# Cross attention: scores of two head pairs issued together between two projections; the last reciprocals pair by pair

## What is computed

```python
q = (x @ Wq).reshape(B, N, 8, 64).transpose(0, 2, 1, 3)          # B = 8, N = 128
k = (context @ Wk).reshape(B, M, 8, 64).transpose(0, 2, 1, 3)    # M = 2048
v = (context @ Wv).reshape(B, M, 8, 64).transpose(0, 2, 1, 3)
attn = softmax(einsum('bhnd,bhmd->bhnm', q, k) * 64 ** -0.5, axis=-1)
out = einsum('bhnm,bhmd->bhnd', attn, v)
out = out.transpose(0, 2, 1, 3).reshape(B, N, 512)
return out @ Wo + bo
```

## Time and profile before

| | |
|---|---|
| median of 3 runs | 1626.52 us (1625.01 to 1626.78) |
| profiled execution, its own time | 1637.39 us |
| its span | 1635.5 us |
| TensorE matmul busy | 1560.3 us, 95% of the span |
| TensorE weight load busy | 1225.8 us, 75% |
| GpSimd busy | 722.9 us, 44% |
| ScalarE busy | 694.3 us, 42% |
| VectorE busy | 630.8 us, 39% |
| mean granted TensorE clock | 0.983 of full speed |

### The profile page before, as it was taken

How to read it: one execution, slowest core, us unless ns; L and a number is a source line. 1 busy time by engine, 2 the same in 40 slices (tenths; PEclk the granted TensorE clock), 3 DMA queues, 4 the chain that set the end, 5 groups by cost and what they waited for, 6 DMA issues and landing times. The chain is left out here.

```text
span 1635.5 us, 25132 instructions
## 1 busy us (share of the span) xinstructions
PE 1560.3 (95%) x10022; PEld 1225.8 (75%) x10023; DVE 630.8 (39%) x951; ACT 694.3 (42%) x1132; POOL 722.9 (44%) x563
## 2 busy tenths in 40 slices
PE   7999999999999999999999999789899969999997
PEld 5677877877878878877877877734467747877876
DVE  4135435434434533533633632641644522222222
ACT  3244544544544544544544543414344403453522
POOL 3113913922931931941841850436200175588651
PEclk9999999999999999999999999999999989999999
DMA  5111021021021021020020110051000465556521
GB/s 206 58 52 59 1 85 57 3 84 44 16 85 33 27 85 33 27 84 31 29 85 26 33 66 27 1 205 64 23 1 1 149 212 135 149 160 191 158 39 35
DMA packets 56164, 116.90 MB, mean 71 GB/s; under 512 B 11072, under 2 KB 15232, under 8 KB 56064
## 3 DMA queue, kind: packets, MB, share of 16 engines
q1 hardware_dynamic: 46480, 98.17, 18.2%
q0 software_dynamic: 4816, 8.41, 2.7%
q10 hardware_dynamic: 4768, 8.91, 1.8%
HBM read 94.19 MB, written 22.33 MB: 71 GB/s over the span
## 5 line engine op out<-in xcount | busy, mean ns | idle before, releaser
L281 POOL TENSOR_TENSOR ctx_l<-stage,ctx_h 128x1024 fp32r<-128x1024 f32 x62 | 147.1, 2393 | 505.4 <-ACT ctx_h L616 505.3
L343 PE MATMUL ps_p<-wv,ctx_h 128*128 128x512 f32 x1024 | 329.3, 403 | 9.5 <-DVE ctx_l L686 9.3
L343 PE MATMUL ps_p<-ctx_h,wk 128*128 128x512 f32 x1024 | 336.2, 397 | 0.0
L724 DVE TENSOR_TENSOR s_top<-ps_s,s_top 128x512 f32<-128x512 f32 x192 | 123.5, 685 | 348.2 <-ACT s L589 348.2
L343 PEld LDWEIGHTS ps_p<-wv,ctx_h 128*128 128x128 f32 x1024 | 185.1, 189 | 56.2 <-issue 10.0
L343 PEld LDWEIGHTS ps_p<-ctx_h,wk 128*128 128x128 f32 x1024 | 192.2, 188 | 44.6 <-issue 2.9
L343 PE MATMUL ps_p<-wv,ctx_l 128*128 128x512 f32 x512 | 201.1, 393 | 0.0
L343 PE MATMUL ps_p<-ctx_l,wk 128*128 128x512 f32 x512 | 199.7, 390 | 0.0
L571 ACT ACTIVATE vt<-ps_p 128x512 f32<-128x512 f32 x128 | 76.4, 597 | 260.6 <-PE ps_p L343 199.4
L565 ACT ACTIVATE kT<-ps_p 128x512 f32<-128x512 f32 x128 | 76.4, 597 | 225.9 <-PE ps_p L343 142.3
L589 ACT ACTIVATE s<-ps_s 128x512 f32<-128x512 f32 x256 | 138.1, 598 | 52.2 <-PE ps_s L396 52.2
(11 more groups left out here) (252 smaller groups left out, 2291.7 us busy)
## 6 DMA issues: line engine op xcount, KB each, us to landing
stage<-in_ctx_dram SPq DMA_DIRECT2D x64, 512.0 KB, 3.9
raw_u<-in_up_dram SPq DMA_DIRECT2D x32, 512.0 KB
stage<-in_down_dram SPq DMA_DIRECT2D x16, 512.0 KB
raw_e<-in_down_dram SPq DMA_DIRECT2D x16, 512.0 KB
rows_scratch<-wxo SPq DMA_DIRECT2D x25, 256.0 KB, 2.6
wxo<-rows_scratch ACTq DMA_DIRECT2D x23, 256.0 KB
s<-in_x_dram SPq DMA_DIRECT2D x2, 1024.0 KB, 11.1
q_scratch<-s SPq DMA_DIRECT2D x2, 1024.0 KB, 4.5
```

Source lines behind the costliest of these rows:

```text
L281: nc.gpsimd.tensor_tensor(lo, raw, hi, ALU.subtract).then_inc(done, 1)
L343: mm = nc.tensor.matmul(out, w(c), m(c), start=(c + k == 0), stop=(c == DC - 1 and k == 2))
L724: ins = nc.vector.tensor_tensor(top[:, p, e], bank, top[:, p, e], ALU.max)
```

## The change

TensorE's `keys_and_scores` and `values_and_scores` take pairs two at a time: two score blocks, then two projections. ScalarE's functions follow. In `keys_and_scores` the scores now also come ahead of the projections. For the last sequence, `sums_of_chunks` writes into `ps_s`, `sums` of heads 0 to 3 is issued after pair 2, and VectorE takes the reciprocals in three steps.

```diff
+            def late_place(h):
+                return ps_s[h % 2 * XD:(h % 2 + 1) * XD, h // 2, 0:T]
...
             def sums_of_chunks(p):
                 for t in range(MT):
                     for h in (2 * p, 2 * p + 1):
-                        nc.tensor.matmul(sum_place(h), ones, s[:, h, t, :], start=(t == 0), stop=(t == MT - 1))
+                        mm = nc.tensor.matmul(late_place(h), ones, s[:, h, t, :], start=(t == 0), stop=(t == MT - 1))
+                mm.then_inc(late_done, 1)
...
             def keys_and_scores(b, g, also=None):
-                for p in range(PAIRS):
-                    project_k(b, g, p)
-                    scores(b, g - 1, p)
-                    if also:
-                        also(p)
+                for q in (0, 2):
+                    for p in (q, q + 1):
+                        scores(b, g - 1, p)
+                    for p in (q, q + 1):
+                        project_k(b, g, p)
+                        if also:
+                            also(p)
 
             def values_and_scores(b, g, also=None):
-                for t in range(4):
-                    scores(b, g, t)
-                    project_v(b, g, t)
-                    if also:
-                        also(t)
+                for q in (0, 2):
+                    for p in (q, q + 1):
+                        scores(b, g, p)
+                    for t in (q, q + 1):
+                        project_v(b, g, t)
+                        if also:
+                            also(t)
...
                 values(LASTB, p)
                 if p >= PAIRS // 2:
                     sums_of_chunks(p)
-            sums(LASTB, range(XH // 2))
+                if p == PAIRS // 2:
+                    sums(LASTB, range(XH // 2))
...
-            output(LASTB)
+            dve.wait_ge(l_done, B)
+            dve.wait_ge(o_stored, 16 * LASTB)
+            nc.vector.reciprocal(on[:, 0:PAIRS // 2, :].rearrange("p h t -> p (h t)"), ps_m[:, 0:PAIRS // 2 * T])
+            for p in range(PAIRS // 2, PAIRS):
+                dve.wait_ge(late_done, p - PAIRS // 2 + 1)
+                ins = nc.vector.reciprocal(on[:, p, :], ps_s[:, p, 0:T])
+            ins.then_inc(r_done, 1)
+            dve.wait_ge(r_done, B)
+            dve.wait_ge(pv_done, B * PAIRS)
+            nc.vector.tensor_tensor(on[:, :, :], ps_o[:, :, :], on[:, :, :], ALU.mult).then_inc(on_done, 1)
```

More of the change, by code:

```diff
@@ L165, in cross_attention @@
         l_done = sem("l_done")
+        late_done = sem("late_done")
         r_done = sem("r_done")
@@ L598, in keys_and_scores @@
             def keys_and_scores(b, g, also=None):
[L599 to L603, removed]
-            def values_and_scores(b, g):
-                for t in range(4):
-                    copy_score(b, g, t)
-                    copy_v(b, g, t)
+                for q in (0, 2):
+                    for p in (q, q + 1):
+                        copy_score(b, g - 1, p)
+                    for p in (q, q + 1):
+                        copy_key(b, g, p)
+                        if also:
+                            also(p)
+            def values_and_scores(b, g):
+                for q in (0, 2):
+                    for p in (q, q + 1):
+                        copy_score(b, g, p)
+                    for t in (q, q + 1):
+                        copy_v(b, g, t)
             def round_ctx(b, ks):
```

## The result

| | median | lowest to highest | ratio to before, 95% interval |
|---|---|---|---|
| before | 1626.65 us | 1625.01 to 1627.98 (4 runs) | |
| changed | 1600.05 us | 1599.48 to 1601.19 (4 runs) | 0.9838 [0.9821, 0.9855] |

The change saves 26.6 us; forecast were 27.2, and a time of 1599.3. The profiled execution of the changed kernel took 1599.48 us, its span 1597.6 us.

The account below looks back on a forecast made before the run. TensorE, busy 1560 of 1635.5 us, was taken as the bound. Savings of 24.1 + 1.3 + 1.35 + 0.4 = 27.2 us from the median 1626.5 gave 1599.3 us, range 1596 to 1608.

Parts of the forecast that it names:

- The gap of a run: Cross attention, TensorE: joining two score blocks saves 0.43 us; 56 joins give 24.1 us.
- The seam behind the values: Seven sequences, scores right behind values matmuls: seam costs 0.15 instead of 0.33 us, saving 1.3 us (0 to 2.3).
- the rule beside it: The Trainium skill's rule that changing tiling mode drains TensorE; by it the values seam saves zero, the sum 1.3 us less.
- The score banks: A pair fills all four banks of `ps_s`; they are emptied with at least 1.9 us spare, costing nothing.
- The tight place: First group: ScalarE's copy of pair 3 waits for GpSimd's last tree; TensorE spared by 0.9 us, cost nothing.
- Rivals A and C: A: tree delay passes cover, 14 us given back, 1613, chance 0.10; C: emptying becomes the bound, 1635, chance 0.03.
- The start of the last softmax: Last sequence: VectorE's first subtraction starts 1.1 us before the transposes instead of 0.27 after, saving 1.35 us.
- Sums and reciprocals: Last sequence: VectorE owes 128 reciprocal elements, not 512, against a new 2.1 us TensorE wait; saves 0.4 us.
- Rival E: Clock falls in the new wait before the last sequence's sums: up to 7.6 us, 1607; counted within the forecast's 0.80.
- Rival B: The gap is partly the recording's: joins give only 12 us, the sum is 15, time 1611; chance 0.05.

Follow-up runs that it names:

- full_pairs: The changed kernel with score matmuls over all 128 rows of keys and queries instead of row halves: 1684.31 us, against 1625.50 for the kernel before.
- fours: The changed kernel with four score blocks, then four value projections, in values_and_scores: 1651.86 us, ratio 1.0156 to the kernel before.
- tree1_after: The changed kernel with one more addition in GpSimd's last tree of each of seven sequences: 1598.05 us, against 1625.12 for the kernel before.
- tree4_after: The changed kernel with four more additions in GpSimd's last tree of each of seven sequences: 1609.82 us.
- tree4_before: The kernel before with four more additions in GpSimd's last tree of seven sequences: 1634.24 us against 1635.94 for the kernel before, ratio 0.999.
- sums_later: The changed kernel with the last sequence's sums of heads 0 to 3 behind the values of pair 3: 1607.02 us, ratio 0.9826 to the kernel before.
- after_again: The changed kernel unaltered, timed again on the slower chip: 1609.12 us against 1635.94 for the kernel before, ratio 0.9841.
- tail_only: The kernel before, score blocks single, with only the changed end of the last sequence (reciprocals in steps, sums after pair 2): 1625.89 us, ratio 1.000.
- keys_first: The changed kernel with two key projections ahead of the two score blocks in keys_and_scores: 1632.99 us against 1625.12 for the kernel before, ratio 1.0046.

## Why the prediction was right, point by point

- **The gap of a run, 24.1 us.** Right in size. The pair period is 7.65 us, and `full_pairs` shows that nothing is saved where the array isn't switched. The argument from the one seam in the kernel before (same waits, no gap) ruled out the waits; that the switch is the cause stands in the prediction only behind its treatment of the seams, and the experiment showed it. One small term was left out: in sequence 0 two joined runs stand behind query matmuls, with a longer gap than the 0.35 us of most others (TensorE's weight loads):

```profile
76.99 1.86 PEld L397 LDWEIGHTS ps_s<-qT,kT 64*128 64x128 f32 x32 [0.76 <-issue]
```

That sequence gave 2.67 us (its values start at 174.94 before and 172.27 after), not 7 x 0.43 = 3.0; I had the queries at nothing.
- **The seam behind the values, 1.3 us.** Right in size, but wrong in what I made of the rule beside it. The first values matmuls of sequence 1 and those of sequence 6, before and then after (TensorE's timelines):

```profile
300.23 0.44 PE L425 MATMUL ps_o<-s,vt 128*64 128x128 f32 x4
...
926.65 0.33 PE L425 MATMUL ps_o<-s,vt 128*64 128x128 f32 x2
```

```profile
294.33 0.43 PE L426 MATMUL ps_o<-s,vt 128*64 128x128 f32 x3
...
904.67 0.33 PE L426 MATMUL ps_o<-s,vt 128*64 128x128 f32 x2
```

Over five sequences that is 125.28 us a sequence before and 122.07 after, 3.21 less; seven joins are 7 x 0.43 = 3.01, leaving 0.20 where I took 0.18, so 1.4 us in place of 1.3. The prediction says that this term is zero if a change from column halves to row halves costs as much as one from the full array. That doesn't follow. Before, the way from values over a projection to scores had two changes; after, the way from values to scores has one. With one price for all changes a change is saved, half of 0.43, 1.5 us in seven sequences. And the trace shows one price at the entry to scores:

```profile
308.25 0.28 PE L426 MATMUL ps_o<-s,vt 128*64 128x128 f32 x2
308.46 0.38 PE L397 MATMUL ps_s<-qT,kT 64*128 64x128 f32 x2
```

From values it takes 0.21 us (308.25 to 308.46, against 0.11 from one pair of values records to the next), from a projection 0.32 (316.98 to 317.30, against 0.23 from one projection record to the next): about 0.1 us of delay in both. In both the second pair of scores records then comes 0.21 us after the first, where later pairs come after 0.11. So count changes of tiling, not runs: a middle sequence has 15 fewer, at 3.21 / 15 = 0.21 us each. The 0.15 us that I read from the sums leaves out the delay behind the first pair of scores, which stands in both orders and so drops out of the difference.
- **The score banks.** No wait of scores for maxima, as forecast; `fours` shows that three blocks in a row bring one.
- **The tight place.** Forecast were a 3 us wait of ScalarE and 0.9 us of cover; there were 3.4 and 0.9. `tree1_after` stays inside the cover, `tree4_after` goes beyond it. Rivals A and C had the right mechanism, and the cover held.
- **The start of the last softmax, 1.35 us.** Measured 8.13 - 6.74 = 1.39.
- **Sums and reciprocals, 0.4 us.** Measured 0.36. TensorE's wait was 1.84 (forecast 2.1), a reciprocal of 128 elements 0.90 to 0.96 (forecast 0.84).
- **Rival E.** The clock stayed up behind the wait of 1.84 us: the stretches around it have a granted clock of 1.00 (the number behind the count of records). It fell in two experiments.

```profile
1026.00:1028.00 2.00, 0.42 (x8) 1.00 0.00 0
1028.00:1030.00 2.00, 1.74 (x32) 1.00 0.00 0
1030.00:1032.00 2.00, 2.00 (x42) 1.00 0.03 8
```

- **Rival B, and the 10.9 us that I carried over.** I gave no reason for the 10.9 us by which the profiled execution before lay above its median, and only carried them over. The profiled execution after lies at its median, and its span is 37.9 us shorter, not 27. From the product to the end of the span it is 1635.5 - 1063.85 = 571.7 us before and 1597.6 - 1036.94 = 560.7 after, in self attention and the experts, which the change doesn't touch. The other profiles tell whose 11 us these are. On the chip on which every kernel took 10 us longer (`tree4_before`, `sums_later`, `after_again`) this rest is 569.3 to 570.0 us, in the eight other experiments 555.8 to 562.3. In the profile before and in these three, the extra time lies in the same stretch of the experts, which starts some 258 us behind the product and ends at 302 to 304, in `tail_only` at 293. So it looks like the chip's own, and not like the recording's or one chance execution's; on which chip the profile before was taken isn't on record, and why that chip is slower there stays open. The cross attention, up to the product, shows 1063.85 - 1036.94 = 26.9 us, the times 26.6, and that is the change. The recording doesn't inflate the gap, so B fell. The forecast time could be right because the 10.9 us have nothing to do with the change; the prediction took that for granted.

## What to carry to other kernels

Matmuls on row halves cost a fixed 0.43 us per run here when they stand among full-array ones, for a run of one block as for one of two; each change of tiling is half of it. So join runs until the banks that they fill run out, and not beyond, since at four blocks the stall (1.8 us, 3.0 in the last group) cost four to seven times what a join saves. Find the price of a join in the old trace, at a place where two such runs already meet. And when work moves forward, look for the one wait that has cover only because the work came late: here GpSimd's tree, whose 3.6 us of slack on ScalarE became a wait, with 0.9 us left for TensorE.

## What was not expected of the hardware

A wait of 2.66 us on TensorE in an otherwise full stream was followed by a granted clock of 0.50, and 32 records then took 3.68 us instead of 2.06 (`keys_first`, once in every sequence). In `fours`, two waits of 1.22 us with 1.2 us of work between them did it in some sequences and not in others. A wait of 1.84 us alone did not, in the changed kernel. So a stall can cost more than its length. And full-array score matmuls cost 0.11 us a record against 0.055 for halves, so the two halves do work side by side: with its switch a lone block in halves (1.32 us) still beats a full-array one (1.80), and a joined one (1.10) more so.
